# Turned batches 4, 5, 7, 8, 10, 11, 13, 14, turned loads on GpSimd's queue, X's low part partly on VectorE, and another order of the drain

## What is computed

```
q, k, v = heads(rgb, wq_rgb), heads(geo, wk_point), heads(geo, wv_point)   # 8 heads of d = 16 channels
attn    = softmax(einsum('bhni,bhnj->bhij', q, k) * d**-0.5)              # n runs over the 1024 positions
res_p2r = einsum('bhnd,bhde->bhne', v, attn) @ proj_p2r.T
res_r2p = the same with rgb and geo, and their weights, swapped
output  = rgb + res_p2r + geo + res_r2p                                   # as (b, channel, position)
```

## Time and profile before

| | before |
|---|---|
| median of 3 runs (range) | 143.73 us (141.33 to 144.34) |
| profiled execution | 139.62 us, span 137.6 us |
| TensorE matmul / weight load busy | 122.6 / 110.8 us |
| VectorE / ScalarE / GpSimd busy | 74.0 / 83.8 / 77.4 us |
| last output matmul ends | 134.4 us into the span |
| data moved | 36.35 MB, mean 264 GB/s |

### The profile page before, as it was taken

One profiled execution on the slowest core, in us unless ns is written; L12 is line 12 of the kernel. 1 busy time (PEld: TensorE's weight loads), 2 busy tenths in 40 slices (PEclk: granted clock), 3 DMA queues, 4 the chain that ended last, 5 costly groups with the idle time before them and its releaser, 6 DMA issues.

```text
span 137.6 us, 2644 instructions
## 1 busy us (share of the span) xinstructions
PE 122.6 (89%) x840; PEld 110.8 (81%) x840; DVE 74.0 (54%) x214; ACT 83.8 (61%) x190; POOL 77.4 (56%) x41
## 2 busy tenths in 40 slices
PE   7947896489999999999999699999999999997780
PEld 7927794387989899989899689898989998976560
DVE  0024227359596861797862387869696173434310
ACT  3013376316695959485953877875795958595321
POOL 5000076943859596729586069595789572959000
PEclk9997799968999999999999999999999999999999
DMA  4899999999999999999999999999944030303124
GB/s 141 229 394 370 268 278 300 315 310 287 405 404 357 362 245 371 355 366 277 199 395 411 361 364 250 210 378 412 413 202 167 26 131 0 152 0 157 61 96 152
DMA packets 18526, 36.35 MB, mean 264 GB/s; under 512 B 1488, under 2 KB 11856, under 8 KB 18512
## 3 DMA queue, kind: packets, MB, share of 16 engines
q1 hardware_dynamic: 13072, 30.94, 68.4%
q10 hardware_dynamic: 5440, 5.24, 13.0%
HBM read 27.79 MB, written 8.39 MB: 263 GB/s over the span
## 4 chain that ended last, share of the span: by engine, by line
PE 63%; DMA 26%; ACT 3%; DVE 2%; SPq 2%; issue 1%; ACTq 1%; DVEq 0%
PE out_ps L298 29%; PE gram_bank L279 15%; DMA gz<-in_ctx_dram 11%; DMA out_dram<-out_sb 10%; DMA w_sb<-in_weights_dram 5%; PE sy_bank L328 4%; PE t_bank L337 3%; PE t_bank L338 2%; PE sy_bank L351 2%; PE sy_bank L350 2%; PE xt_ps L258 2%; PE gt_ps L258 2%; ACT out_sb L370 1%; PE uv_bank L318 1%; PE uv_bank L320 1%
## 5 line engine op out<-in xcount | busy, mean ns | idle before, releaser
L194 POOL TENSOR_TENSOR x_lo<-x_raw,x_hi 128x1024 fp32r<-128x1024 f32 x16 | 38.0, 2378 | 42.6 <-ACT x_hi L363 42.6
L197 POOL TENSOR_TENSOR g_lo<-g_raw,g_hi 128x1024 fp32r<-128x1024 f32 x16 | 38.0, 2376 | 6.0 <-ACT g_hi L363 6.0
L279 PE MATMUL gram_bank<-gt,xt 128*128 128x128 f32 x256 | 35.2, 282 | 0.0
L279 PEld LDWEIGHTS gram_bank<-gt,xt 128*128 128x128 f32 x256 | 32.4, 199 | 0.0
L370 ACT COPY out_sb<-out_ps 128x512 f32<-128x512 f32 x32 | 18.5, 581 | 9.4 <-PE out_ps L298 4.1
L395 ACT ACTIVATE expd<-scores,min_neg 128x128 f32<-128x128 f32 x32 | 12.6, 395 | 8.0 <-DVE min_neg L457 8.0
L363 ACT CAST g_hi<-g_raw 128x1024 fp32r<-128x1024 f32 x16 | 16.9, 1058 | 0.0
L363 ACT CAST x_hi<-x_raw 128x1024 fp32r<-128x1024 f32 x16 | 16.6, 1035 | 0.0
L444 DVE COPY gt<-gt_ps 128x512 f32<-128x512 f32 x12 | 8.2, 688 | 15.2 <-PE gt_ps L258 15.2
L298 PE MATMUL out_ps<-x_hi,t_hi 128*128 128x512 f32 x32 | 14.4, 450 | 1.4 <-ACT t_hi L423 1.4
L484 DVE COPY y_sb<-sy_bank 128x256 f32<-128x256 f32 x16 | 6.7, 422 | 16.5 <-PE sy_bank L328 16.5
(11 more groups left out here) (49 smaller groups left out, 205.1 us busy)
## 6 DMA issues: line engine op xcount, KB each, us to landing
x_raw<-in_x_dram SPq DMA_DIRECT2D x15, 512.0 KB, 14.8
g_raw<-in_ctx_dram SPq DMA_DIRECT2D x15, 512.0 KB, 15.0
out_dram<-out_sb SPq DMA_DIRECT2D x15, 512.0 KB, 11.9
xz<-in_x_dram SPq DMA_DIRECT2D x10, 256.0 KB, 10.3
gz<-in_ctx_dram SPq DMA_DIRECT2D x10, 256.0 KB, 12.6
xz<-in_x_dram ACTq DMA_DIRECT2D x10, 256.0 KB, 13.3
gz<-in_ctx_dram ACTq DMA_DIRECT2D x10, 256.0 KB, 14.6
x_raw<-in_x_dram SPq DMA_DIRECT2D x2, 256.0 KB, 3.8
```

Source lines behind the costliest of these rows:

```text
L194: nc.gpsimd.tensor_tensor(x_lo[:, slot, :], x_raw[:, raw_slot, :], x_hi[:, slot, :].bitcast(F32), ALU.subtract).then_inc(x_lo_ready, 1)
L197: nc.gpsimd.tensor_tensor(g_lo[:, slot, :], g_raw[:, raw_slot, :], g_hi[:, slot, :].bitcast(F32), ALU.subtract).then_inc(g_lo_ready, 1)
L279: last = nc.tensor.matmul(gram_ps, xt[:, b % 2, cols], gt[:, b % 2, cols], start=(t == 0), stop=(t == TILES - 1))
```

## The change

1. `VECTOR_PAIRS` has four pairs: (4,5), (7,8), (10,11), (13,14). Batches 3, 6, 9 and 12 are now turned by TensorE with 0, 1, 2 and 15; before it was 0, 1, 2, 7, 10 and 15.
2. SP issues all four quads of pair 0, behind plain load 3. For pairs 1 to 3, quads 2 and 3 are issued by GpSimd ahead of the low parts of batches 1, 4 and 7; ScalarE issues no DMA.
3. X's low part of batches 0, 1, 4, 7, 10, 13, 14 and 15 is made by VectorE, in the steps where it transposes nothing, behind its copy of G's first half and ahead of the identity's addition. GpSimd makes the other eight, and all of G's.
4. `out_sb` has four slots. `t_hi` and `t_lo` have two buffers.
5. 42 warm matmuls in place of 56. `wu_hi` is made at the end of ScalarE's step 1, `wu_lo` in VectorE's step 2.
6. Drain: batch 13's second output half and batch 14's first stand behind batch 15's scores, batch 14's second half is cut into three and three matmuls around batch 15's `t`, and ScalarE copies those second halves behind `t_hi`.

```diff
-OUT_SLOTS = 3
+OUT_SLOTS = 4
-WARM = 56
+WARM = 42
-VECTOR_PAIRS = ((3, 4), (5, 6), (8, 9), (11, 12), (13, 14))
+VECTOR_PAIRS = ((4, 5), (7, 8), (10, 11), (13, 14))
...
+        lo_on_vector = [b for b in range(B) if b + 2 in on_tensor or b + 2 >= B]
+        lo_on_pool = [b for b in range(B) if b not in lo_on_vector]
+        def x_lo_made(eng, b):
+            if b in lo_on_vector:
+                eng.wait_ge(x_lo_vector_ready, lo_on_vector.index(b) + 1)
+            else:
+                eng.wait_ge(x_lo_ready, lo_on_pool.index(b) + 1)
...
# GpSimd
+            issued_at = {1 if pair < PAIRS else VECTOR_PAIRS[pair - PAIRS][1] - 1: pair
+                         for pair in range(1, len(VECTOR_PAIRS))}
             for b in range(B):
+                pair = issued_at.get(b)
+                if pair is not None:
+                    if pair >= PAIRS:
+                        pair_turned(pool, pair - PAIRS)
+                    load_turned(pool, x_turn, xz, xz_pool_loaded, pair, (2, 3))
                 if b >= SPLIT_SLOTS:
                     pool.wait_ge(half_done, 2 * (b - SPLIT_SLOTS) + 2)
-                pool.wait_ge(x_hi_ready, b + 1)
-                nc.gpsimd.tensor_tensor(x_lo[:, slot, :], ...).then_inc(x_lo_ready, 1)
+                if b in lo_on_pool:
+                    pool.wait_ge(x_hi_ready, b + 1)
+                    nc.gpsimd.tensor_tensor(x_lo[:, slot, :], ...).then_inc(x_lo_ready, 1)
+                if pair is not None:
+                    load_turned(pool, g_turn, gz, gz_pool_loaded, pair, (2, 3))
...
# SP
-            load_turned(sp, x_turn, xz, xz_loaded, 0, (0, 1))
-            load_turned(sp, g_turn, gz, gz_loaded, 0, (0, 1))
             load_plain(3)
+            load_turned(sp, x_turn, xz, xz_loaded, 0, (0, 2, 1, 3))
+            load_turned(sp, g_turn, gz, gz_loaded, 0, (0, 2, 1, 3))
+            load_plain(4)
             load_turned(sp, x_turn, xz, xz_loaded, 1, (0, 1))
             load_turned(sp, g_turn, gz, gz_loaded, 1, (0, 1))
-            load_plain(4)
             load_plain(5)
...
-                    sp.wait_ge(x_lo_ready, i - 2)
+                    x_lo_made(sp, i - 3)
...
# TensorE: last_half(b, half) becomes last_parts(b, half, first=0, end=6), with w[:, b % 2, which, :]
                 if l >= 0:
-                    last_half(l, 0)
-                    last_half(l, 1)
+                    if l != B - 2:
+                        last_parts(l, 0)
+                    if l < B - 3 or l == B - 1:
+                        last_parts(l, 1)
...
+                if i == B + 2:
+                    last_parts(B - 2, 1, 0, 3)      # behind y
...
+                if i == B + 2:
+                    last_parts(B - 2, 1, 3, 6)      # behind t
...
+                if i == B + 1:
+                    last_parts(B - 3, 1)            # behind s
+                    last_parts(B - 2, 0)
...
# ScalarE: both load_turned loops go; wu_hi moves from i == 0 to the end of i == 1
-                    if y >= 1:
-                        act.wait_ge(half_done, 2 * y)
+                    if y >= 2:
+                        act.wait_ge(half_done, 2 * y - 2)
...
# VectorE, between copy_gt(i, 0) and the identity's addition
+                if i - 2 in lo_on_vector:
+                    dve.wait_ge(x_hi_ready, i - 1)
+                    if i - 2 >= SPLIT_SLOTS:
+                        dve.wait_ge(half_done, 2 * (i - 2 - SPLIT_SLOTS) + 2)
+                    nc.vector.tensor_tensor(x_lo[:, (i - 2) % SPLIT_SLOTS, :], ...).then_inc(x_lo_vector_ready, 1)
```

More of the change, by code:

```diff
@@ L106, in bass_cross_channel_attention @@
         gz_loaded = [sem(f"gz_loaded{s}") for s in range(PAIRS)]
+        xz_pool_loaded = [sem(f"xz_pool_loaded{s}") for s in range(PAIRS)]
+        gz_pool_loaded = [sem(f"gz_pool_loaded{s}") for s in range(PAIRS)]
         x_loaded = [sem(f"x_loaded{s}") for s in range(RAW_SLOTS)]
@@ L282, in gram_half, with last_parts @@
                     last.then_inc(gram_done, 1)
-            def last_half(b, half):
+            def last_parts(b, half, first=0, end=6):
                 slot = b % SPLIT_SLOTS
@@ L289, in last_half @@
                     pe.wait_ge(t_hi_ready, b + 1)
-                if b >= 1:
+                if first == 0 and b >= 1:
                     pe.wait_ge(half_copied, 2 * (b - 1) + 1 + half)
-                for n, (w, which, moving) in enumerate(parts):
+                for n in range(first, end):
+                    w, which, moving = parts[n]
                     if half == 0 and n == 2:
-                        pe.wait_ge(x_lo_ready, b + 1)
+                        x_lo_made(pe, b)
                         pe.wait_ge(g_lo_ready, b + 1)
@@ L297, in last_half @@
                         pe.wait_ge(t_lo_ready, b + 1)
-                    last = nc.tensor.matmul(out_ps[:, cols], w[:, which, :], moving[:, slot, cols], start=(n == 0),
+                    last = nc.tensor.matmul(out_ps[:, cols], w[:, b % 2, which, :], moving[:, slot, cols], start=(n == 0),
                                             stop=(n == len(parts) - 1))
-                last.then_inc(half_done, 1)
+                if end == len(parts):
+                    last.then_inc(half_done, 1)
             pe.wait_ge(warm_ready, 1)
@@ L401, in _ @@
                     evacuate(l, 0)
-                for pair in range(len(VECTOR_PAIRS)):
-                    if i == (1 + pair if pair < PAIRS else VECTOR_PAIRS[pair - PAIRS][1] + 1):
-                        load_turned(act, g_turn, gz, gz_loaded, pair, (2, 3))
-                if l >= 0:
+                if l >= 0 and l not in (B - 3, B - 2):
                     evacuate(l, 1)
@@ L413, in _ @@
                     copy_xt(i, 0)
-                if i == 0:
-                    act.wait_ge(wu_loaded, 16)
-                    nc.scalar.copy(wu_hi[:, :, :], w_sb[:, WQR:WKR + 1, :]).then_inc(wu_hi_ready, 1)
                 if 0 <= s < B:
```

55 lines of the change are left out of this document (32 added, 23 removed).

## The result

| | before | changed |
|---|---|---|
| median of 6 runs each (range) | 142.53 us (140.10 to 144.34) | **150.66 us** (149.40 to 153.07) |
| profiled execution, span | 139.62, 137.6 us | 153.07, 151.2 us |
| TensorE matmul busy | 122.6 us | 125.3 us |
| data moved | 36.35 MB, 264 GB/s | 34.26 MB, 227 GB/s |

The ratio is 1.077, 95% interval 1.069 to 1.084: slower, where 138.4 was forecast. Ratios here leave out disturbed executions, so they can differ a little from the quotient of two medians, and where too few are left none is given.

The account below looks back on a forecast made before the run. TensorE's matmuls were busy 89% of the span, with the DMA engines busy nearly throughout up to slice 31. Sum: 139.62 - 5.4 + 0.5 - 0.3 - 1.5 + 3.5 = 136.4 us, plus 2.0 gives 138.4; range 133.5 to 143.5.

Parts of the forecast that it names:

- The start: Up to step 4: batch 0's `uv` at 14.5 instead of 17.37, step 4 at 25.6 instead of 30.98, -5.4 us.
- the one on the loads: Within steps 4 to 16: 8 MB of turned loads against 10, so loads less pressed; no size of its own.
- Loads decide: Rival, chance 0.10: plain load 6 lands at 41 for step 6's transposes, up to 3 us more, 141.4 us.
- Pair 0: Step 4: the pair's last data may come late for VectorE, between 0 and 1.5 us, taken as +0.5.
- VectorE's `x_lo`: Tensor steps: `x_lo` waits for GpSimd's `g_lo`, TensorE loses 1.7 us per step; two steps (12, 15), +3.5 us.
- the threshold of 1.25: Steps 6 and 9: if one GpSimd issue takes longer than 1.25 us, VectorE is first and GpSimd waits instead.
- GpSimd late: Rival, chance 0.10: from step 6, issues over 3.0 us make `g_lo` late for output matmuls; up to 19 us more, 157.
- The drain: From step 17 to the end: new order cuts idleness from 3.5 to 2.1 us, -1.5, so 16.2 us.
- Steps 4 to 16 otherwise: Eight turned steps, step 16 and four tensor steps take 88.6 us instead of 88.94; fourth slot eases step 10; -0.3.
- The 2.0 us added for the distance between profiled execution and median: Whole kernel: half of the 4.1 us by which the runs' median lay above the profiled execution, added to 136.4.

Follow-up runs that it names:

- experiment 14: Kernel before with only the new drain order, two buffers for `t_hi` and `t_lo` and four output slots: 140.18 us, ratio 0.996.
- experiment 2: Changed kernel with quads 2 and 3 of pairs 1 to 3 issued by ScalarE instead of GpSimd, pair 0 still SP alone: 146.46 us, ratio 1.031.
- experiments 4 and 5: Kernel before: in 4 GpSimd issues quads 2 and 3 in place of ScalarE, 149.51 us, ratio 1.043; in 5 SP issues all four quads, 142.95 us.
- three fixes: Changed kernel, all pairs split between SP and ScalarE, `g_lo` waiting for VectorE's `x_lo`, pair 1 behind load 6: 140.16 us; again 142.56, ratio 1.017.
- experiment 6: Changed kernel with all pairs split between SP and ScalarE, quads 0 and 2 on SP, 1 and 3 on ScalarE: 146.02 us, ratio 1.033.
- Two fixes: Changed kernel, all pairs split between SP and ScalarE, pair 1 a step earlier, `g_lo` waiting for VectorE's `x_lo`: 137.7 us, ratio 0.970.

## Why the prediction was wrong, by its steps

**The start was right.** Batch 0's `uv` came at 14.53 (forecast 14.5). Within that forecast no run shows by itself what it takes off for a slow stretch of the clock, up to 1.6 us; what the traces show is a granted clock of 0.50 from 12 to 15 us before (0.54 over all of 11.5 to 15), and of 1.00 from 8 to 23 us in the changed kernel. Step 4 began at 25.19 in place of 30.63 on the timeline: 5.4 us, as forecast.

**The step that failed** is the one on the loads: "8 MB against 10 MB, so the loads are less pressed than before". By it the sum has no term for the plain loads. The rival *Loads decide* had the right mechanism and place, but was priced at 3 us at most and given 0.10. The bytes weren't the term, the rate was. The rival has 12 MB from 2 us on at 324 GB/s, so load 6 landed by 41 at the latest; it landed at 53.54. The 2 us to land in it, like the 1.5 in the term for pair 0, were my estimate, and no row shows them; in the kernel before, plain loads of 512 KB took 6.0 to 20.2 us from issue to landing, and a last store of 256 KB 2.0. I took 324 from a stretch of one execution of the kernel before in which SP and ScalarE issued side by side. The same loads moved 276 from 14 to 38 us in experiment 14, and load 6 landed at 44.2. And when the change took ScalarE out I priced only the length of an issue.

What the runs show in its place: GpSimd's queue cost 6 us of load 6's lateness (53.5 against 47.4, experiment 2), by the rate after 38 us; experiments 4 and 5 show the same in the kernel before. The rest, 47.4 in place of 41, isn't GpSimd's: two hardware queues had 231 and 255 GB/s from 26 to 38 us as well, and with pair 1 behind load 6 it landed at 37 to 39. Put into the sum, the 232 GB/s of 14 to 38 us give 53.7, but that fits by luck: up to 53.5 us the DMAs moved 256 GB/s, 13.7 MB and not 12. Among the rest were quads of pair 2, which GpSimd had issued from 40.26 on in a queue of its own; two of them landed ahead of load 6.

It cost 13.3 us in step 6: not a wait of 10 alone, but 10 and a slow clock behind it, 3.3. My rival had step 6 without that clock.

**Pair 0** was forecast at +0.5 and cost +1.5: step 4 took 7.77 in place of 6.28.

**VectorE's `x_lo` was right in mechanism, and one of its prices was off.** It waits for the whole of `g_lo`, 3.22 us in all where 3.15 was worked out (56.0 to 59.15). Three meetings of 2 us show it: in steps 9, 12 and 15 `x_lo` takes 3.22, 3.29 and 3.28 us and ends 1.08 to 1.09 behind `g_lo`'s end, with `g_lo` undisturbed at 2.35 to 2.36. It holds the other way round too: where `x_lo` was first, at 22.86, `g_lo` began at 23.10 and took 3.22, and nothing waited for it. Per tensor step 1.7 us was forecast, and 1.71, 1.78 and 1.77 were lost (the step and the one after it, less 8.03 + 6.28). But the number of steps was off: GpSimd's issue takes 0.58 us, not 1.5, so below the threshold of 1.25. Its four issues end at 76.46 and GpSimd is idle until `g_hi`:

```profile
L157 POOL DMA_DIRECT2D xz<-in_x_dram x6: 583/584/739, 20.1 to 74.7; - x6
L157 POOL DMA_DIRECT2D gz<-in_ctx_dram x6: 583/583/586, 21.4 to 75.9; - x6
```

SP's issues took up to 4.59 us before and up to 5.7 now; GpSimd's never did. That a full queue makes an issue long was a guess of mine that no row shows. Three steps waited, 5.3 us in place of 3.5. Step 6 would have been the fourth, but GpSimd made its `g_lo` at 52.56, during the wait for load 6, and `x_lo` at 56.59 took 1.22. The rival *GpSimd late* fell with it: its condition was an issue over 3 us.

**The drain** was forecast at -1.5 and gave -0.5. Both drains, from the first output matmul of step 17 on the timeline to the last one's end:

```profile
119.68:134.45 14.77, 12.31 (x62) 9.56 (x60) 5.11 (x20) 7.59 (x19) 5.78 (x3) 1.00 0.18 73
```

```profile
133.89:148.14 14.25, 12.30 (x62) 9.15 (x60) 6.19 (x21) 7.38 (x20) 3.97 (x2) 1.00 0.19 75
```

The work is the same, 12.3 us, and the idleness fell from 14.77 - 12.31 = 2.46 to 14.25 - 12.30 = 1.95. The new order was forecast well: pauses of 0.5, 0.45, 0.8 and 0.3 us, and 0.36, 0.52, 0.80 and 0.23 came. What failed is the old order's idleness, 3.5. I had added up 11.0 us of work from durations of an unbroken stretch, where the chain leaves out the quarter of a microsecond by which a group overlaps the one ahead. Behind a pause there is no such overlap. With four pauses in the drain, before and now, most of the 1.3 us that were missing is this, and I had taken it for idle time that a new order could fill.

**Steps 4 to 16 otherwise** were forecast at -0.3 and gave -0.4. The number is right, and part of its ground isn't: with four slots alone (experiment 14) a load took the store's place in step 10.

**The account.** Forecast for an execution like the profiled one, 136.4; measured 153.07. Step 6 +13.3, pair 0 +1.0, `x_lo` +1.8, drain +0.9, steps otherwise -0.1, start 0.0, outside the span -0.2: 16.7, as it should be.

The 2.0 us added for the distance between profiled execution and median had no ground: before's own median was 142.53 with six runs, the changed kernel's profiled execution lay above its median and not below, and the two runs of three fixes show scatter that comes with the rate of the DMAs.

**Open.** Why GpSimd's queue lowers the rate of all. Its transfers are in other partitions than SP's, as ScalarE's were, and the packets it moved were larger (960 for 3.15 MB, against 5440 for 5.24 MB on ScalarE's queue before), so neither the place nor small packets explain it; whether larger packets take more than their share wasn't tried. It isn't work of VectorE or GpSimd either, which both stood still from 46 to 50 us at 246 GB/s. Why two hardware queues fall to 231 to 255 GB/s from 26 to 38 us when pair 1 stands ahead of load 6 is open too. Why one kernel has 321 GB/s in one execution and 291 in another isn't settled either.

## What to carry to other kernels

Before a move of transfers from one queue to another, read the GB/s of the stretch, not the DMA share (311 and 232 GB/s here at 1.08 and 1.09), and ask who works beside whom in which partitions (297 and 215 GB/s in experiment 6); then put the new rate, not the old one, into the sum for the first load that is needed. Take that rate from more than one execution. A load that comes late costs its wait and the clock behind it (here 10 and 3.3 us). And don't add up work from an unbroken stretch to find out how much of a broken one is idle. Of this change only the early start with the turned loads kept on SP and ScalarE may be worth keeping. Two fixes had a ratio of 0.970, the two kernels with `x_lo` left to GpSimd 0.984 and 0.987, but three fixes 1.017. Only 0.984 has an interval below 1 (0.969 to 0.998), and as one of thirteen kernels, with an end so near 1, that isn't shown to be a gain.

## What the runs showed of the hardware that I had not expected

- Turned loads of 32 partitions each, among plain ones, from 14 to 26 us: two hardware queues on different halves 309 to 315 GB/s where pair 1 stands ahead of load 6, 267 to 316 where it doesn't, and 252 to 285 in the order of the kernel before; quads 0 and 2 on one and 1 and 3 on the other 255; pair 0 on SP alone 238 to 260; SP with GpSimd 232 (experiment 4). The DMA share was 1.07 to 1.12 in all of them, so it says nothing of the rate.
- An issue of such a load took GpSimd 0.58 us, also while SP stood for microseconds in its own (12 issues, 0.583 to 0.739), where SP's of the same shape took 0.33 to 5.7 in the changed kernel.
- A VectorE subtraction of two SBUF operands and one of GpSimd took turns in the changed kernel, whichever was first: `x_lo` 3.22 to 3.29 us in place of 1.22 behind `g_lo`, `g_lo` 3.22 in place of 2.35 behind `x_lo`.
- A pause cost TensorE about 0.25 us more than its idle time, at full clock (1.44 and 1.51 us of idleness, 1.69 to 1.76 lost), since the overlap with the group ahead is gone; the work behind it isn't slower (twelve output matmuls in 3.08 us behind a pause, 3.06 without).
